# Latent attention on one Trainium2 core: each unit's weighing as one piece of TensorE's work in place of two halves, with new ranks for the planner

## What is computed

```python
xn = _layernorm(x)
q = einsum('bld,dhk->blhk', xn, Wq)                  # 16 heads of 64
latent = einsum('bld,dc->blc', xn, Wkv_down)         # 64 wide
k = einsum('blc,chk->blhk', latent, Wk_up)
v = einsum('blc,chk->blhk', latent, Wv_up)
attn = softmax(where(causal, einsum('bqhd,bkhd->bhqk', q, k) / 8, -inf))
s = einsum('bqhd,hdo->bqo', einsum('bhqk,bkhd->bqhd', attn, v), Wout)
g = silu(local_network(xn, ...))
out = x + s * g
```

## Time and profile before

| | us |
|---|---|
| median of 3 runs | 2292.62 |
| lowest, highest | 2284.94, 2297.12 |
| the profiled execution's own time | 2309.97 |
| its span, first to last instruction | 2308.2 |
| PE busy in the span | 2036.0 |
| DVE busy | 1755.4 |
| POOL busy | 1519.6 |
| ACT busy | 1307.2 |
| mean granted TensorE clock | 0.945 of full |

### The profile page before, as it was taken

The page is one execution under the profiler, slowest core; times in us unless marked ns, Lnnn a source line. Parts: engine busy times, 40 slices in busy tenths (PEclk is TensorE's granted clock), DMA queues, the critical chain, the costliest instruction groups (busy, mean ns, idle before and its releaser), DMA issues. The chain is left out here.

```text
span 2308.2 us, 44944 instructions
## 1 busy us (share of the span) xinstructions
PE 2036.0 (88%) x15232; PEld 1601.3 (69%) x15232; DVE 1755.4 (76%) x3171; ACT 1307.2 (57%) x3178; POOL 1519.6 (66%) x1385
## 2 busy tenths in 40 slices
PE   6578999999899999999998788989897999899985
PEld 4457777777677777777776576767676767676764
DVE  5687877777878887778686258988788888888883
ACT  3256567666666566667664265545554565466541
POOL 2465665657646655576564138988888889888983
PEclk9689999999999999999998789999999999999998
DMA  8333333333233323333332216787678777877685
GB/s 271 95 99 91 92 87 82 99 88 95 71 101 94 107 76 92 88 96 85 77 91 75 83 31 154 190 200 181 164 190 199 182 176 186 204 179 179 180 206 131
DMA packets 189459, 298.26 MB, mean 129 GB/s; under 512 B 52360, under 2 KB 97328, under 8 KB 188208
## 3 DMA queue, kind: packets, MB, share of 16 engines
q1 hardware_dynamic: 171568, 254.99, 42.7%
q10 hardware_dynamic: 10752, 21.51, 3.6%
q0 software_dynamic: 6912, 18.89, 3.2%
HBM read 56.13 MB, written 20.97 MB: 33 GB/s over the span
## 5 line engine op out<-in xcount | busy, mean ns | idle before, releaser
L2068 POOL TENSOR_TENSOR g_ring<-g_ring,g_rl 128x768 f32<-128x768 f32 (+6 forms) x168 | 384.6, 2302 | 44.8 <-DVE g_rl L2009 39.9
L1158 POOL TENSOR_TENSOR l_pb<-l_pb,l_rl 128x1024 f32<-128x1024 f32 (+1 forms) x128 | 229.4, 1792 | 252.9 <-DVE l_rl L1018 252.9
L1897 ACT ACTIVATE g_ring<-ps,g_mx 128x128 f32<-128x128 f32 (+7 forms) x384 | 273.6, 726 | 200.5 <-DVE g_mx L1991 91.4
L1784 PE MATMUL ps<-g_turned,g_latV 128*64 128x256 f32 (+1 forms) x1984 | 297.1, 446 | 72.3 <-issue 38.2
L873 ACT ACTIVATE l_pb<-ps,l_mx 128x256 f32<-128x256 f32 (+1 forms) x512 | 228.5, 464 | 143.5 <-DVE l_mx L1010 143.4
L2016 DVE STREAM_TRANSPOSE g_ring<-g_ring 128x896 f32<-128x896 f32 (+4 forms) x264 | 256.9, 997 | 15.5 <-POOL g_ring L2068 15.1
L1784 PEld LDWEIGHTS ps<-g_turned,g_latV 128*64 128x64 f32 x1984 | 149.7, 145 | 164.4 <-issue 100.4
L1010 DVE CUSTOM_DVE_ANT_0 ps<-ps,l_mask 128x256 f32<-128x256 f32 (+1 forms) x512 | 188.2, 438 | 10.5 <-PE ps L707 10.5
L1174 POOL TENSOR_TENSOR l_act_lo<-l_u,l_act_hi 128x512 fp32r<-128x512 f32 x80 | 104.8, 1310 | 132.0 <-ACT l_act_hi L923 132.0
L112 PE MATMUL ps<-l_wqkv_hi,l_x_hi 128*128 128x512 f32 x384 | 171.4, 446 | 14.3 <-POOL l_x_lo L1128 13.6
L112 PE MATMUL ps<-l_h_hi,l_w_hi 128*128 128x512 f32 (+1 forms) x352 | 147.4, 419 | 38.9 <-DVE l_h_lo L1063 32.6
(11 more groups left out here) (208 smaller groups left out, 6312.4 us busy)
## 6 DMA issues: line engine op xcount, KB each, us to landing
l_pt<-l_pb SPq DMA_DIRECT2D x1024, 64.0 KB, 2.0
g_turned<-g_ring SPq DMA_DIRECT2D x192, 112.0 KB, 2.9
g_turned<-g_ring SPq DMA_DIRECT2D x140, 128.0 KB, 3.7
g_turned<-g_pt SPq DMA_DIRECT2D x140, 128.0 KB, 3.5
g_turned<-g_ring SPq DMA_DIRECT2D x184, 96.0 KB, 2.8
g_turned<-g_ring SPq DMA_DIRECT2D x192, 80.0 KB, 2.4
g_turned<-g_pt SPq DMA_DIRECT2D x96, 96.0 KB, 2.2
l_tab<-turns SPq DMA_DIRECT2D x64, 128.0 KB, 2.2
```

The costliest lines, as they stand in the source:

```text
L1158: pool.tensor_tensor(view, view, rl[:, g % 2, h, :].unsqueeze(2).unsqueeze(3).to_broadcast([P, 4, NB, n // NB]), ALU.mult).then_inc(s["sca ...
L1784: last = pe.matmul(o, latV[:, b % 2, c, :], turned[:, :, a, c, :, :], start=(c == 0), stop=(c == t), skip_group_check=True)
L1897: act.activation(to, some, ACT.Exp, bias=mx[:, u % 2, at:at + 1], accum_out=sm[:, u % 2, at:at + 1]).then_inc(s["ex"], 1)
L2068: pool.tensor_tensor(view, view, some, ALU.mult).then_inc(s["scaled"], 1)
```

## The change

The planner's COST and RANK tables are replaced. A weighing becomes one event `("weigh", u)` on TensorE, with a cost of 0.3 + (t + 1) x 0.44 or 0.91 in the model where the halves had 0.1 each beside it. All that needed the second half now needs the whole. The matmuls and their order within a weighing stay.

```diff
-    COST = (2.798, 3.485, 2.704, 3.109, 4.273, 4.971, 2.906, 5.516)
+    COST = (3.123, 3.865, 2.715, 3.109, 4.132, 4.979, 2.135, 5.808)
     RANK = {
-        "pe": {"latent": -47.82, "values": -24.02, "query": -31.9, "scores": -25.01, "weigh": 9.04, "wout": 45.42,
-              "back": -30.97},
-        "act": {"split_x": -19.34, "latent": -49.22, "values": -35.13, "query": -28.2, "exp": -41.46, "evacuate": -31.16,
-              "gate": -1.39, "move": 6.07},
-        "dve": {"latent": -25.65, "query": -42.67, "largest": 2.95, "share": -44.35, "blocks": 55.82, "gate": 57.15,
-              "back": -10.55},
-        "pool": {"split_x": -58.63, "scale": -23.93, "divide": 15.42, "move": -11.05},
-        "sp": {"xn": 15.62, "f": 2.67, "x": 19.26, "move": 14.3, "store": 45.53},
+        "pe": {"latent": -35.35, "values": -24.24, "query": -34.28, "scores": -25.56, "weigh": 11.37, "wout": 36.16,
+              "back": -18.5},
+        "act": {"split_x": -19.55, "latent": -65.56, "values": -40.83, "query": -27.36, "exp": -32.11, "evacuate": -38.06,
+              "gate": 8.0, "move": 14.89},
+        "dve": {"latent": -31.8, "query": -40.12, "largest": 3.91, "share": -40.32, "blocks": 62.44, "gate": 92.97,
+              "back": -8.46},
+        "pool": {"split_x": -90.61, "scale": -23.15, "divide": 16.86, "move": -27.79},
+        "sp": {"xn": 3.08, "f": -26.99, "x": 12.7, "move": 14.37, "store": 36.48},
     }
...
-                  "weigh": [("weigh", u, i) for u in range(U) for i in range(2 if self.units[u][1] else 1)],
+                  "weigh": [("weigh", u) for u in range(U)],
...
         if kind == "weigh":
             t = self.units[n][1]
-            some = 1 if t == 0 else (t + 2) // 2 if event[2] == 0 else t + 1 - (t + 2) // 2
-            return 0.1 + some * (0.44 if t >= self.LONG else 0.91)
+            return 0.3 + (t + 1) * (0.44 if t >= self.LONG else 0.91)
...
-            out += [("pe", ("weigh", n - 2, 1 if self.units[n - 2][1] else 0))] if n >= 2 else []
+            out += [("pe", ("weigh", n - 2))] if n >= 2 else []
...
-                def weigh(u, i, bank):
+                def weigh(u, bank):
...
-                    some = range(t + 1) if t == 0 else range((t + 2) // 2) if i == 0 else range((t + 2) // 2, t + 1)
-                    if i == 0:
-                        pe.wait_ge(s[f"pt{u % SLOTS_G}"], 16 * moved(u))
...
+                    pe.wait_ge(s[f"pt{u % SLOTS_G}"], 16 * moved(u))
...
-                    for c in some:
+                    for c in range(t + 1):
...
-                    if some[-1] == t:
-                        last.then_inc(s["pv"], 1)
+                    last.then_inc(s["pv"], 1)
```

More of the change, by code:

```diff
@@ L1381, in needs @@
         elif kind == "evacuate":
-            out += [("pe", ("weigh", n, 1 if self.units[n][1] else 0))] + ([("pool", ("divide", n - 2))] if n >= 2 else [])
+            out += [("pe", ("weigh", n))] + ([("pool", ("divide", n - 2))] if n >= 2 else [])
         elif kind == "divide":
@@ L1400, in needs @@
                 v = self.unit_of[n - NZ] - 1
-                out += [("pe", ("weigh", v, 1))]
+                out += [("pe", ("weigh", v))]
         elif kind == "query":
@@ L1486, in ready @@
             times.append(done[need])
-        if engine == "pe" and not (event[0] in ("weigh", "wout") and event[2]):
+        if engine == "pe" and not (event[0] == "wout" and event[2]):
             banks = self.room(event, free, now)
@@ L1631, in attend_g @@
                 "query": lambda z, i: ("qlo", GP // 2 * z + i + 1), "exp": lambda k, a: ("ex", heads[k] + a + 1),
-                "weigh": lambda u, i: ("ev", u + 1), "wout": lambda z, m: ("prod", z + 1), "back": lambda z: ("y", z + 1)}
+                "weigh": lambda u: ("ev", u + 1), "wout": lambda z, m: ("prod", z + 1), "back": lambda z: ("y", z + 1)}
         with nc.Block() as block:
@@ L1768, in half @@
                         last.then_inc(s["sc"], 1)
-                def weigh(u, i, bank):
+                def weigh(u, bank):
                     b, t, r = units[u]
-                    some = range(t + 1) if t == 0 else range((t + 2) // 2) if i == 0 else range((t + 2) // 2, t + 1)
-                    if i == 0:
-                        pe.wait_ge(s[f"pt{u % SLOTS_G}"], 16 * moved(u))
[L1776 to L1779, removed]
+                    pe.wait_ge(s[f"pt{u % SLOTS_G}"], 16 * moved(u))
+                    pe.wait_ge(s[f"own{u % SLOTS_G}"], 16 * kept(u))
+                    if below(u):
+                        pe.wait_ge(s[f"sub{u % SLOTS_G}"], 16 * below(u))
+                    pe.wait_ge(s["v"], tile(u)[0] + 1)
                     turned = PT[:, u % 2, :, 0:run(u)].rearrange("p i (h a r q) -> p h a r i q", a=2, r=t + 1, q=32)
-                    for c in some:
+                    for c in range(t + 1):
                         for a in range(2):
@@ L1821, in _ @@
                     elif e[0] == "weigh":
-                        weigh(e[1], e[2], plan.bank[e])
+                        weigh(e[1], plan.bank[e])
                     elif e[0] == "wout":
@@ L1935, in _ @@
                     elif e[0] == "evacuate":
-                        evacuate(e[1], plan.bank["weigh", e[1], 0])
+                        evacuate(e[1], plan.bank["weigh", e[1]])
                     elif e[0] == "move":
```

## The result

The changed kernel takes 2308.12 us (median of 9 runs, 2295.67 to 2317.91) beside 2293.66 us for the kernel before on the same chip (9 runs, 2284.94 to 2297.78): the ratio is 1.0053, 95% interval 1.0034 to 1.0073. A later comparison gave 1.0051 (1.0027 to 1.0075). So it is slower by half a per cent, 12 us by the ratio, where the prediction said 12 us faster. The profiled execution took 2308.20 us, with a span of 2306.4.

A forecast was written before the change was run, and what follows sets the result against it. It took TensorE, stalled in the attention before weighings whose data SyncE's moves bring late, as the bound. Terms -2 + 4 + 2 - 15 - 1 = -12 us from the median 2292.62 gave 2280 us; range 2256 to 2314.

The forecast's parts named there:

- The ranks: Latent attention: weighings ranked one score pair later fill a bit under a third of 53 us of body stalls, -15 us.
- POOL's ranks: POOL: the move's two issues now go in front of a scaling; taken as 0, ends -5 and +10 us.
- Scores kept waiting behind a whole weighing: TensorE: score steps from between the halves wait for the second half, mostly covered by VectorE's transposes; +4 us, upper end 30.
- `pv` earlier: 24 parted units: joining halves lets `pv` rise earlier for SyncE's moves; -2 us, ends 0 and -34.
- The end: Kernel's end, unit 92's weighing: a score step waits for the other 12 matmuls without cover; +2 us, ends 0 and +3.
- The clock: TensorE in the attention: fewer stalls give back a little of the granted clock, -1 us.
- Coarseness: Rival: half of 30 us for scores behind whole weighings is paid, ranks give nothing; +15 us, 2308, chance 0.08.
- The ring: Rival: later weighings raise `pv` later, delaying SyncE's moves at each group's third unit; +17 us, 2310, chance 0.19.
- Nothing: Rival: stalls move from one weighing to the next, since SyncE's issuing sets data arrival; 2286 to 2297, chance 0.26.
- That filling stalls would then gain nothing: TensorE: by load share it has 30% to spare, so filling stalls gains nothing, sum +6 less 2; prediction sided against this.

The follow-up runs named there:

- e12_halves_new_ranks: The kernel before with its halves, given the changed kernel's COST and RANK and planned anew; ratio 1.0278 against before.
- h2_whole_searched: The changed kernel's code with whole pieces and its costs, with a RANK table of its own from a random search; ratio 1.0043 against before.
- e11_whole_old_ranks: The changed code with whole pieces, given the COST and RANK of the kernel before and planned anew; ratio 1.0182 against before.
- g3_old_pool_ranks: The changed kernel with only POOL's row of RANK put back to that of before; ratio 1.0241 against the kernel before.
- e1_joined: The kernel before with the 24 parted second halves moved up behind their first halves on TensorE, all other orders kept; ratio 1.0062.
- e9_latent_joined: The kernel before with only the second halves of units 20, 44 and 68, between `latent` and `values`, moved up behind their first; ratio 1.0058.
- g1_last_two_joined: Changed kernel's tables and whole pieces up to about unit 68, those of before after it, with units 87 and 92 also joined; 1.0054 against before.
- h1_halves_searched: The kernel before with its halves and costs, with a RANK table of its own from a random search; 2282.83 us, ratio 0.9945.
- e6_all_but_seams: The kernel before with 18 of the 24 parted units joined, the six at the seams between batches left as before; ratio 1.0037.
- e8_before_again: The kernel before, unchanged, run once more for a second profile; ratio 1.0002 against before.

## Why the prediction was wrong

**The ranks, -15 us: the step that failed.** The prediction read the ranks one engine at a time, found "one score pair later" for a weighing on TensorE, and took a bit under a third of the 53 us of body stalls as filled. The weighing's waits went from 68.4 to 65.0 us, outside the 45 to 60 it named. Nor were they a gauge of the time: e12_halves_new_ranks has 58.7 us of them and h2_whole_searched 48.9, and the two are 64 and 10 us slower than before. e11_whole_old_ranks, e12_halves_new_ranks and the changed kernel show in its place that the table has no worth by itself: -30 us with whole pieces, +64 with halves. Beside the whole pieces it repairs part of what they break. "What the ranks are worth no row can tell, for the order is worked out by the planner" is true of the rows, but the planner could be asked: its own model ends 10.9 us later with the change.

**POOL's ranks, 0 (-5 to +10).** g3_old_pool_ranks shows 43 us on POOL's row. The prediction priced the move alone. It does not mention `split_x`, which goes from 34.7 to 67.5 us ahead of the scaling, and how the 43 us divide between the row's numbers is open. The error was to ask what the engine would do first where both are ready, for POOL by itself; what a rank changes is the schedule from which all five lists are written.

**Scores kept waiting behind a whole weighing, +4 (0 to +30), and `pv` earlier, -2 (0 to -34).** e1_joined measures both together with the end at +14 us, against +4 in the sum: the size was missed. The cover that the prediction counted on, VectorE's transposes, did not hold: VectorE's search waits for scores grew from 80.2 and 68.8 us to 93.8 in e1_joined. Whether that is the whole of the 14 us is not shown. SyncE's wait for a weighing fell little by joining alone (28.9 us) and to 16.0 in the changed kernel; it gave nothing, since SyncE there waits for the transposes. The prediction also took "what stood between the halves" as the only thing displaced. In three places it was the half that was the filler (e9_latent_joined: 1.45 us idle, then 62 matmuls in 6 us in place of 84).

**The end, +2 (0 to +3).** Whole weighings there do cost, as it said, but more: 8 us by the runs for units 87 and 92 (g1_last_two_joined), of which the prediction counted only 92. The profiles show 2.4 us of it or none, so the path is not confirmed.

**The clock, -1.** Wrong sign. With some 7 us more idle time TensorE's busy time rose by some 7 (means of two profiles each). The Trainium skill ("TensorE: Matmul & The Clock Gate", Why this matters for your kernels) says to avoid idle gaps between bursts of matmuls, against a drop of the throughput. The traces agree and go further: the page has longer gaps in mind than the 1.45 us behind which the clock fell in eight of nine places. A long piece doesn't make gaps fewer.

**The rivals.** Coarseness (2308, given 0.08) has the measured time, in part by luck. It is borne out by e1_joined, +14 us, and by the search's waits, though not in the row that it named (34.8 and 43.2 us, not over 55) but in the sum of all rows. But it took the ranks to give nothing, where whole pieces planned by the old table cost 42 us and the new table takes 30 of them back. The ring (2310, 0.19) is refuted: SyncE's wait for a weighing fell. "Nothing" had its sign, the weighing's waits nearly unchanged, without its time. The Trainium skill ("Perfetto Trace Analysis", Identifying the Most-Contended Engine) says that TensorE's matmul busy time misleads about its headroom and that the load share should be used. That filling stalls would then gain nothing was the prediction's own step, and h1_halves_searched does not bear it out: its loads are busy 656 of 933 us, its waits ahead of weighings are 21 us or more below those of before, and it is 13 us faster by the ratio.

The time, 2308, lay in the range of 2256 to 2314, whose upper end came from the rivals and not from the forecast's own sum. The chance of 0.42 for faster did not come in, that of 0.23 for slower did.

## What to carry to other kernels

Where one planner writes all engines' lists, pieces and ranks are one setting: never cost a new table as a term beside the edit it comes with, but ask the planner's own model first (here it says +10.9 us where +12 was measured), and then measure the two by two of pieces and tables, which takes two more runs. Before joining two pieces of work, look at what the second piece itself hides (here ScalarE's copy between `latent` and `values`), since even a short stall of TensorE may cost more than its length. Cut profiles at events of the work, not at fixed times, and profile a kernel twice before reading from profiles a difference as small as the scatter between two of them, here 13 us.

## What the runs showed of the hardware

An idle gap of only 1.45 us on TensorE, at three places of the work, stood ahead of 6 us at a granted clock of 0.61 to 0.72 in eight of nine cases (e1_joined, e6_all_but_seams, e9_latent_joined), where the nine cases without the gap had 1.00. Over the whole attention the same 7552 matmuls were busy for 833.5, 842.7 and 866.0 us at 0.96, 0.95 and 0.92 with idle times of 105.7, 115.9 and 147.4 us (e8_before_again, the changed kernel, e12_halves_new_ranks). The two do not go in step: e11_whole_old_ranks is busy 850.4 us with 136.0 idle, and h1_halves_searched 842.5 with 90.5. And two profiled executions of the same kernel differed by 13 us in the attention, 7.4 of it in TensorE's busy time (840.87 and 833.50 us).
